# Second layer's front: the order of a turn changed on three engines, GpSimd's products given to VectorE

## The reference

```python
h = layernorm(x) * (1 + ca) + sa
q, k, v = (silu(conv4(h @ W, w)) for W, w in ((Wq, conv_q), (Wk, conv_k), (Wv, conv_v)))
mix = sigmoid(rot_logit)                      # one number per head, 4 heads of 64
q = mix * rotary(q, sin, cos) + (1 - mix) * q
k = mix * rotary(k, sin, cos) + (1 - mix) * k
beta, gamma = sigmoid(h @ Wb), sigmoid(h @ Wgamma)
q, k = l2norm(q), l2norm(k); v = v * beta; kb = k * beta
A = -(kb @ k.T) * strict_lower                # in chunks of 32 rows
frac = rmsnorm(fractal_mixer(h, frac_conv_w), mixer_norm_w)
x = x + ga * (core + sigmoid(h @ frac_gate_w + b) * frac)   # core comes from the recurrence
```

## Time and profile before

| what | value |
|---|---|
| median of 3 runs | 3036.22 us (3028.84 to 3037.94) |
| the profiled execution's own time | 3033.11 us |
| its span in the trace | 3031.3 us |
| this stage, first to last | 2257.0 to 2639.3 us of the span |
| PE, DVE, ACT, POOL busy over the span | 88%, 75%, 52%, 12% |

### The profile page before, as it was taken

How to read it: one execution, slowest core, us unless ns; L and a number is a source line. 1 busy time by engine, 2 the same in 40 slices (tenths; PEclk the granted TensorE clock), 3 DMA queues, 4 the chain that set the end, 5 groups by cost and what they waited for, 6 DMA issues and landing times. The chain is left out here.

```text
span 3031.3 us, 92578 instructions
## 1 busy us (share of the span) xinstructions
PE 2655.4 (88%) x35848; PEld 1616.0 (53%) x35848; DVE 2270.6 (75%) x4339; ACT 1581.4 (52%) x2164; POOL 370.5 (12%) x340
## 2 busy tenths in 40 slices
PE   6879999899989998999999978999987777309997
PEld 3322556656656774567556624555545555306774
DVE  3449899789879897999889914555546987685777
ACT  2320677677767776777677772211116666304442
POOL 1246000000000000000000110000001222202333
PEclk8985899999999999999999988999998887759998
DMA  4253011101110111101110001000000222313342
GB/s 134 83 104 75 3 27 28 26 6 26 27 28 11 20 27 27 27 6 26 27 27 7 4 18 51 14 28 14 14 2 26 71 80 87 107 37 105 107 117 66
DMA packets 130637, 130.32 MB, mean 43 GB/s; under 512 B 76418, under 2 KB 107780, under 8 KB 125060
## 3 DMA queue, kind: packets, MB, share of 16 engines
q1 hardware_dynamic: 124548, 120.93, 17.0%
q10 hardware_dynamic: 4224, 4.19, 0.4%
q0 software_dynamic: 1536, 0.40, 0.1%
HBM read 78.41 MB, written 46.66 MB: 41 GB/s over the span
## 5 line engine op out<-in xcount | busy, mean ns | idle before, releaser
L697 DVE TENSOR_REDUCE attn_pm<-attn_MS 128x1 f32<-128x512 f32 (+3 forms) x2304 | 1334.4, 639 | 171.5 <-PE attn_MS L741 144.8
L681 ACT ACTIVATE attn_PT<-attn_ES 128x1024 f32<-128x1024 f32 (+5 forms) x1152 | 1038.8, 951 | 372.2 <-PE attn_ES L776 369.8
L791 PE MATMUL attn_OP<-attn_PT,attn_VH 128*17 128x512 f32 (+3 forms) x4608 | 650.3, 563 | 0.3 <-ACT attn_PT L681 0.2
L741 PE MATMUL attn_MS<-head_KX,head_QX 96*32 96x512 bf16 (+11 forms) x3456 | 395.7, 393 | 5.6 <-DVE attn_pm L697 3.5
L741 PE MATMUL attn_MS<-after_attention,attn_QX 96*32 96x512 bf16 (+8 forms) x2880 | 333.7, 358 | 4.2 <-issue 3.0
L776 PE MATMUL attn_ES<-head_QX,head_KX 99*32 99x512 bf16 (+8 forms) x3456 | 286.9, 368 | 42.9 <-issue 21.8
L741 PE MATMUL attn_MS<-attn_KX,attn_QX 96*32 96x512 bf16 (+7 forms) x2880 | 316.7, 369 | 1.3 <-DVE attn_pm L697 1.1
L776 PE MATMUL attn_ES<-attn_QX,attn_KX 99*32 99x512 bf16 (+9 forms) x2880 | 246.1, 357 | 5.9 <-ACT attn_PT L681 4.4
L776 PE MATMUL attn_ES<-attn_QX,after_attention 99*32 99x512 bf16 (+11 forms) x2880 | 242.1, 359 | 4.6 <-ACT attn_PT L681 4.3
L1180 PE MATMUL l0out_ring<-l0out_w,l0out_sT 128*128 128x512 f32 x512 | 224.9, 592 | 0.0
L741 PEld LDWEIGHTS attn_MS<-head_KX,head_QX 96*32 96x32 bf16 x3456 | 156.1, 97 | 122.8 <-DVE attn_pm L697 60.0
(11 more groups left out here) (290 smaller groups left out, 3572.8 us busy)
## 6 DMA issues: line engine op xcount, KB each, us to landing
vk_beta<-front_vk SPq DMA_DIRECT2D x8, 1024.0 KB, 3.9
kq_transposed<-l0out_w_in SPq DMA_DIRECT2D x8, 1024.0 KB, 4.5
delta_VK<-vk_beta SPq DMA_DIRECT2D x32, 256.0 KB, 2.8
delta_QK<-kq_transposed SPq DMA_DIRECT2D x32, 256.0 KB, 2.9
attn_QX<-qk_parts SPq DMA_DIRECT2D x60, 128.0 KB, 7.6
head_KX<-qk_parts SPq DMA_DIRECT2D x36, 128.0 KB, 6.4
head_QX<-qk_parts SPq DMA_DIRECT2D x36, 128.0 KB, 7.1
after_attention<-attn_out SPq DMA_DIRECT2D x18, 256.0 KB
```

What stands on the lines that cost most here:

```text
L681: nc.scalar.activation(PT[u % NPT][:, 512 - wa:512 + wb], ES[half][:, 512 - wa:512 + wb], ACT.Exp, scale=DH ** -0.5).then_inc(exp_done, 1)
L697: nc.vector.tensor_reduce(pm[r][:, i, c:c + 1], MS[slot][:, 0:w], AX.X, ALU.max).then_inc(max_taken, 1)
L741: last = nc.tensor.matmul(MS[slot][r, 0:seen], QX[b][0:ROWS, i * P + 32 * g:i * P + 32 * g + 32], KX[b][0:ROWS, 512 * c:512 * c + seen], s ...
L791: last = nc.tensor.matmul(OP[32 * j:32 * j + DH + 1, 512 - w:512], VH[b][:, kt, :], PT[(2 * n + half) % NPT][:, o:o + w], start=(kt == 0), ...
```

## The change

The same values are computed. The edits are these.
- VectorE's turn is written anew. `mask_products` of a group moves into the next turn (a fourth flag, `three`), behind the first tap of the convolution; `mixer_out` moves from the next turn to the end of its own; `statistics` of group n+1 stands at the end of turn n. The stage has eleven turns on VectorE, the last with `mask_products` alone.
- TensorE and ScalarE do the projections 0 and 1 of group n at the end of turn n, not at the head of turn n+1, and projections 2 and 3 follow directly on the first turned tile.
- ScalarE's SiLUs 0 to 3 stand behind the rates, ahead of the norm's square root; SiLUs 4 and 5 stay behind the turned tiles. The table of functions is switched four times a turn, not three times.
- GpSimd keeps the copy of beta alone. Its sum into `x_res` (`fx`), `m2` and `kb` go to VectorE. The three products with `mix` are gone: the load repeats each table for the 4 heads (8 DMAs of 64 KB a group in place of 2), and VectorE multiplies by `mix` in the last step of the rotation, four scalar-tensor-tensor instructions of 128x512 in place of one sum of 128x2048.
- SP stores the turned heads ahead of the chunk products.

```diff
             def load(g):
-                tiles = bass.ds(g * J, J)
-                sp.dma_start(cs[:, 0, :, :], cos_v[:, tiles, :]).then_inc(csl, 16)
-                sp.dma_start(cs[:, 1, :, :], sin_v[:, tiles, :]).then_inc(csl, 16)
+                for i, table in enumerate((cos_v, sin_v)):
+                    for j in range(J):
+                        sp.dma_start(cs[:, i, j, :, :], table[:, bass.ds(g * J + j, 1), :].broadcast_to([P, HB, 32]))\
+                            .then_inc(csl, 16)
...
                 if g + 1 < G:
-                    sp.wait_ge(bod, BO(g, "cos2"))
+                    sp.wait_ge(bvd, BV(g, "to_1"))
                     load(g + 1)
...
             def turn(n, b, zero, one, two):
 
-                if one:
-                    halo(n - 1)
-                for m in range(6):
-                    if two and m < J:
+                for m in range(4):
+                    if two:
                         take_heads(n - 2, m)
                     if two and m == J - 1:
                         own_share(n - 2)
                     if one:
-                        take_projection(n - 1, m)
+                        for p in ((2, 3), (), (4,), (5,))[m]:
+                            take_projection(n - 1, p)
                 if one:
                     rates(n - 1)
-                if two:
-                    head_squares(n - 2)
+                    for m in range(4):
+                        silu(n - 1, m)
                 if zero:
                     spread(n)
                 if two:
+                    head_squares(n - 2)
                     head_spread(n - 2)
                 if one:
                     mixer_squares(n - 1)
                     mixer_spread(n - 1)
                 if zero:
                     modulate(n, b)
-                if one:
-                    for m in range(4):
-                        silu(n - 1, m)
                 if two:
                     for j in range(J):
                         take_turned(n - 2, j)
                 if one:
                     for m in range(4, 6):
                         silu(n - 1, m)
+                if zero:
+
+                    halo(n)
+                    for m in range(2):
+                        take_projection(n, m)
...
+                xt = x_res[:, bass.ds(g * J, J), :]
+                dve.wait_ge(avd, AV(g, "frx"))
+                dve.sem_inc(held, 1)
+                nc.vector.tensor_tensor(xt, xt, fx[:], ALU.add).then_inc(avd, 1)
...
-                nc.vector.tensor_tensor(XR[:].rearrange("p a j h c -> p (a j h c)"),
-                                        XR[:].rearrange("p a j h c -> p (a j h c)"),
-                                        te[:].rearrange("p a n i c -> p (a n i c)"), ALU.add).then_inc(bvd, 1)
+                dve.sem_inc(held, 1)
+                for h in range(HB):
+                    own = XR[:, :, :, h, :].rearrange("p a j c -> p (a j) c")
+                    turned = te[:].rearrange("p a (j h) i c -> p h (a j) (i c)", h=HB)[:, h, :, :]
+                    last = nc.vector.scalar_tensor_tensor(own, turned, mix[:, h:h + 1], own, ALU.mult, ALU.add)
+                last.then_inc(bvd, 1)
...
+            def turn(n, zero, one, two, three, following):
+
+                if one:
+                    convolve(n - 1, 0, (0,))
+                if three:
+                    mask_products(n - 3)
+                if one:
+                    convolve(n - 1, 0, (1, 2))
                 if two:
                     take_values(n - 2, 0)
-                    mixer_out(n - 2)
+                if one:
+                    convolve(n - 1, 2, (0,))
+                if two:
                     take_values(n - 2, 1)
-                if zero:
-                    statistics(n)
                 if one:
-                    convolve(n - 1, 0)
+                    convolve(n - 1, 2, (1, 2))
                 if two:
                     take_values(n - 2, 2)
                     take_values(n - 2, 3)
                     rotate(n - 2)
+                if zero:
+                    normalise(n)
                 if one:
-                    convolve(n - 1, 2)
+                    convolve(n - 1, 4, (0,))
                 if two:
                     square_sums(n - 2)
                 if one:
-                    convolve(n - 1, 4, (0,))
-                if zero:
-                    normalise(n)
+                    convolve(n - 1, 4, (1,))
                 if two:
                     norms(n - 2)
                 if one:
-                    convolve(n - 1, 4, (1, 2))
+                    convolve(n - 1, 4, (2,))
                 if two:
-                    mask_products(n - 2)
+                    scaled_keys(n - 2)
+                    mask_factors(n - 2)
+                if one:
+                    mixer_out(n - 1)
+                if following:
+                    statistics(n + 1)
...
-            def project(g, b, m):
+            def project(g, b, m, before=None):
                 if m == 0:
                     pe.wait_ge(zad, ZA(g, "hT_1"))
+                if before == "turned":
+                    pe.wait_ge(bad, BA(g - 2, f"qkT_{m + 2}"))
+                if before == "rates":
+                    pe.wait_ge(aad, AA(g - 1, "sig"))
...
                     for j in range(J):
                         turn_rotated(n - 2, j, not one)
+                if zero:
+                    for m in range(2):
+                        project(n, b, m, "turned" if two else "rates" if one else None)
+                if two:
                     for j in range(J):
                         square(n - 2, j)
```

More of the change, by code:

```diff
@@ L1588, in rotate @@
                 dve.wait_ge(bad, BA(g, "X_3"))
-                dve.wait_ge(bod, BO(g, "cos2"))
+                dve.wait_ge(csl, 128 * g + 128)
+                dve.sem_inc(held, 1)
                 Xp = X[:].rearrange("p a j h (c t) -> p a (j h) t c", t=2)
-                turns = csm[:].rearrange("p i j h c -> p (j h) i c")
-                for half, part, slots in ((0, te, slice(0, 2)), (1, to, slice(1, 3))):
+                table = cs[:].rearrange("p i j h c -> p (j h) i c")
+                for half, part in ((0, te), (1, to)):
@@ L1598, in rotate @@
                 dve.wait_ge(bvd, BV(g, "to_1"))
[L1599 to L1600 removed]
+                dve.sem_inc(held, 1)
+                nc.vector.tensor_tensor(ev[:, :, 0, :], ev[:, :, 0, :], od[:, :, 1, :], ALU.subtract).then_inc(bvd, 1)
+                nc.vector.tensor_tensor(ev[:, :, 1, :], ev[:, :, 1, :], od[:, :, 0, :], ALU.add).then_inc(bvd, 1)
@@ L1762, in turn @@
             def turn(n, b, zero, one, two):
-                for m in range(6):
-                    if two and m < J:
+                for m in range(4):
+                    if two:
                         turn_heads(n - 2, m)
                     if one:
-                        project(n - 1, 1 - b, m)
+                        for p in ((2, 3), (), (4,), (5,))[m]:
+                            project(n - 1, 1 - b, p)
                 if one:
```

104 lines of the change are left out of this document (44 added, 60 removed).

## The result

| | before | after |
|---|---|---|
| median of 4 runs | 3033.65 us | 3014.39 us (3013.39 to 3019.29) |
| profiled execution, own time | 3033.11 us | 3019.29 us |
| its span | 3031.3 us | 3017.5 us |
| the stage, first table load to first DMA behind it | 382.01 us | 366.83 us |
| five full turns, mean | 43.07 us | 41.00 us |

The ratio is 0.9945, with an interval of [0.9932, 0.9959]. Predicted were 3021 us and a turn of 40.7. The stage is the steadier measure: what lies outside it took 2641 to 2654 us in the profiled runs of this study, without an edit there, so I compare stages and turns from here on. Each is read from one profiled execution.

What follows compares the result with a forecast made beforehand. No engine is full; waits in a loop through three engines and GpSimd's held-up taps bound it. Five turns 11.9, fill 2 and drain 0.8 make 14.7 us less: 3018.4 profiled, 3021 forecast as median, range 3014 to 3028 (60%).

Steps and rivals of the forecast that it cites:

- Five turns: The five full turns of the stage: from 43.07 to 40.7 us each, 11.9 us less together.
- Fill: The stage's start up to the first `A`: 2 us earlier, with a range of 0 to 4.
- Drain: The two draining turns: 36.4 for 38.51 and 30.8 for 29.46 us, 0.8 us less together; nothing behind the last `A`.
- New work of VectorE: Per turn on VectorE: products, sum and last rotation step +3.3 us, hand-overs at six places +0.6 us.
- The low price: `kb` and the sum cost 1.15 us each on VectorE; at the upper price, GpSimd's times, 2.7 us more.
- The wait for `G` is gone: VectorE's wait of 4.2 us a turn ahead of `A` goes, with `G` done at 8.7 and `A` starting at 9.8.
- GpSimd's held-up taps, -3.4: VectorE's convolution taps, held up while GpSimd runs its products, get 3.4 us a turn shorter once those products go.
- Waits for `pre_2`, `pre_3`, 0.9 and 1.1: Behind `A`, VectorE waits 0.9 and 1.1 us a turn for projections 2 and 3, done in series.
- Projection 0 at the low clock, +0.9: At the seam, low-clock projection 0 makes `pre_0` and `pre_1` 1.7 us later against 0.8 slack: +0.9 us in most turns.
- ScalarE's fourth table load, and the loads: A fourth table load of 1.28 us a turn and eight DMA issues in place of two add nothing to the path.
- Rival 2: TensorE's clock stays low through projections 0 and 1 to the chunk products: 42.4 us a turn, 3034 us; chance 15%.
- Rival 3: Projections 2 and 3 behind `A` run at the low clock: 45.8 us a turn, 3050 us; chance 8%.

Runs made afterwards that it cites:

- e1: The changed kernel with ScalarE's SiLUs 0 to 3 put back behind the modulation, three table loads a turn: 44.48 us a turn, ratio 1.0052.
- e5: The kernel before with only SiLUs 0 to 3 moved ahead of the norm's square root: 39.72 us a turn, ratio 0.9933.
- e2: The changed kernel with `kb`, `m2` and the sum into `x_res` back on GpSimd: 41.03 us a turn, ratio 0.9948.
- e3: The changed kernel's work on its new engines, in the order of before on TensorE, ScalarE and VectorE: 44.10 us a turn, ratio 1.0028.
- e9: e3 with SiLUs 0 to 3 ahead of the norm's square root: 40.79 us a turn, ratio to before 0.9960.
- e4: The changed kernel with projection 2 ahead of heads 0 on TensorE and ScalarE: 39.43 us a turn, ratio 0.9927.
- e6: The changed kernel with 40 discarded transposes on TensorE between the halves of the turned-over rows: 41.54 us a turn, ratio 0.9960.
- e10: The changed kernel with each table load issued a second time into a spare tile: 41.01 us a turn, ratio 0.9947.
- e7: e2 with the 40 discarded transposes of e6: 40.79 us a turn, ratio to before 0.9953.
- e11: e8 with the 40 discarded transposes of e6: 39.47 us a turn, ratio to before 0.9900.
- e8: e2 and e4 together, products on GpSimd and projection 2 ahead of heads 0: 39.27 us a turn, ratio to before 0.9914.

## Why the prediction was right, and where its account was not

The sum: 14.7 us less were forecast, the profiled span shows 13.8 and the stage 15.2 (outside it the profiled execution took 1.4 us more). The medians differ by 19.3. The 3.1 us that I put between the profiled execution and the median was not borne out: the profiled execution took 3019.29 us for 3018.4 forecast, and the median lies 4.9 below it.

- **Five turns**: 11.9 forecast, 10.3 measured (41.00 for 40.7 a turn).
- **Fill**: 2 forecast (0 to 4). From the first table load to the first `A` it is 84.72 for 88.32 us: 3.6.
- **Drain**: 36.4 and 30.8 forecast, 36.01 and 31.42 measured, together 0.5 less than before in place of 0.8. Behind the last `A` 9.66 for 10.39 us, 0.7 that I had at nothing.
- **New work of VectorE**: `kb` and the sum 1.22 each for 1.15, `m2` 0.68 for 0.6, the last rotation step +0.45 for +0.4, hand-overs 0.56 for 0.6. Busy and hand-overs make 36.98 for 36.9 (37.2 less the 0.3 of gaps in it). The low price was right.
- **The wait for `G` is gone**: right, with `A` behind a tap and no wait for `G` in any full turn. The stated cause (SiLUs done earlier, so the second pair does not wait) is shown by e1 and e5. Its weight was not right: it stood as one bullet among others, and it is the gain. e5 has it alone and gains 17.4 us of stage; e1 lacks it alone and loses 24.2.
- **GpSimd's held-up taps, -3.4**: the size was near (taps 12.63 a turn for 12.18, so 2.96 went), and the new work of 3.3 took it back, as the sum had it. That `kb`, `m2` and the sum gain nothing by the move is shown by e2 (41.03 for 41.00). In the order of before the move, together with the tables and the mix, costs (e3 against before +8.9 us of stage, e9 against e5 +3.4).
- **Waits for `pre_2`, `pre_3`, 0.9 and 1.1**: 0.92 and 0.96 measured. e4 shows that they were real and could be had. **Other waits** were mis-sized: the fourth tile 0.7 for 0.4, the root 0.3 for 0.1, `pre_0` and `pre_1` 0.5 on average for 0, most of it (2.1 us) in the last turn, and gaps 0.6 for 0.3.
- **Projection 0 at the low clock, +0.9**: this step failed. I took a whole projection at the low clock, 1.7 us. The two took 4.16 us for 3.60 at the full clock, 0.56 more. Counted from the end of the norms, `pre_0` and `pre_1` were there at 8.3 and 9.4 us (9.2 and 10.3 by the sum at the low clock), and VectorE's own work brings it to these taps at 8.7 and 9.4. So in four of the five turns nothing hangs on the clock there: e6 ran at 1.00 with a turn of 41.14. Only the last turn, without statistics, gave 1.28 us back at 1.00, which is 0.26 a turn. The other terms fell short by 1.3 us together, that 0.26 included, and the 0.9 covered for them, so 40.7 was near 41.0 partly by luck.
- **ScalarE's fourth table load, and the loads**: free, as forecast. e10 shows it for the loads. For the table load, e5 has four a turn and gains; what the extra load costs by itself no run shows. The Trainium skill ("ScalarE: Activation LUTs", What ACT_TABLE_LOAD costs) adds a drain of about 1380 ns to a switch; in e5 the first SiLU starts 1.30 us behind the load's start and the load 1.93 us behind the start of the squares of 1.91 us, so no drain shows on either side.
- **Rival 2**, the low clock up to the chunk products, did not come either: these ran at 1.00 (1.45 us).
- **Rival 3**, projections 2 and 3 at the low clock, did not come in the changed kernel, where TensorE waited 1.4 to 1.7 us for `A` and the clock stayed at 1.00. e6, with waits of 2.5 to 3.0 us there, shows in three of five turns that it is real; e7 and e11 show one such turn each.
- **Slips in the working**: the low-clock case is 40.6 and I took 40.7 for "most turns", where the mean can't be above the case. Rival 2's 3034 should be 3032 by its own terms (3036.2 less 3.4 and 0.8). VectorE's work at its upper price, 2.7 more, would give 43.4 a turn and not rival 2's 42.4. None of them moves the forecast by more than 0.5 us.

What stays open: what the tables and the mix on VectorE cost by themselves, since every run in which they stand apart from before has at least one other part changed; and why the new order only exchanges waits with the SiLUs early in both (e9 and after), which is read from the traces and was not tested further. Open too is which of e4, e8 and e11 is the best kernel: their intervals overlap, and for e4 and e8 the stages (356.17 and 357.35) and turns (39.43 and 39.27) point opposite ways.

## What to carry to other kernels

When a change moves many things, look for the single wait that ends the loop between the engines, ask which one instruction stands in it, and try the move of that instruction alone: here a few lines on ScalarE gave what the whole rewrite gave. Work that is held up beside a wait costs nothing, and freeing it by giving the other engine's work to the same engine gained nothing here, neither with the wait (e3) nor nearly without it (e9). A faster TensorE that then waits for its consumer can lose its clock and give the time back in the next piece of work. Here filler ahead of the wait lost (e6, 5 us of stage), the next useful product in the place of the wait gained (e4, e8: the clock was 1.00 around `A` in all five turns), and both together gained nothing clear over the product alone (e11).

## What the runs showed of the hardware

- A VectorE product of 128x4 elements with both inputs in SBUF took 0.81 us in place of 0.17 beside a GpSimd product, so the hold-up follows the other engine's instruction and not the size of one's own.
- The length of the last wait did not tell TensorE's clock. In e6, behind full-clock work, the products started at 0.50 after waits of 2.47 and 2.99 us; after one of 2.89 us they started at 1.00 and fell to 0.50 some 1 us later; after one of 2.65 us the clock stayed at 1.00. The same 40 transposes kept it at 1.00 at one place and cost it at another, in some turns and not in others.
- Doubling 0.5 MB of table loads a group, in DMAs of 64 KB, moved no other engine by a measurable time.
